# A decoder layer on one core: four pipeline stages instead of five, with the router in attention's iteration

## The chip, the cores and the metric

The kernel runs on one core of one Trainium2 chip. The metric is the device time of one execution in microseconds (us); smaller is better. The engines are PE (TensorE, matmuls), ACT (ScalarE), DVE (VectorE), POOL (GpSimd) and SP (SyncE, which issues all DMAs here). Each engine works through its own list of instructions in order; they meet at semaphores.

## The reference

For 16 batches of 512 tokens with 512 channels, three post-layernorm sublayers follow each other. The linear attention sums along the tokens; the cross attention is one over channels (scores of 128x128 channels in each of 4 heads, twice, with "global" and "local" weights); the feed-forward picks one of 8 experts for a whole batch from the mean of its tokens.

```python
# L0_attn: q, k, v = split(x @ Wqkv.T + bqkv); q, k = elu(scale * .) + 1
denom = clip(einsum('bthd,bthd->bth', q, cumsum(k)), 1e-3)
y = q * cumsum(k * v) / denom
x = layernorm(x + y @ Wproj.T + bproj)
# L0_xattn, for both sets of weights: q = x*wq + bq, k = ctx*wk + bk, v = ctx*wv + bv
scores = einsum('bhdn,bhen->bhde', qh, kh) * 512 ** -0.5
att = einsum('bhde,bhen->bhdn', softmax(scores), vh)
x = layernorm(x + 2.0 * (att_global + att_local) * wp + bp)
# L0_ffn
top1 = argmax(x.mean(axis=1) @ Wr + br)          # one expert for a batch
h = relu(x @ W1[top1] + b1[top1])                # 512 x 2048
x = layernorm(x + h @ W2[top1] + b2[top1])
```

## The kernel before, in words

All products of the linear attention and the feed-forward are split: an operand is a high part (fp32r, copied by ACT) and a low part (the difference, by DVE), and a product of 128 contraction rows is three matmuls hi*hi, hi*lo, lo*hi of 128x512. A group of 12 such matmuls makes one `qkv` job, one `project` tile, one `up` or one `down`.

The kernel is a software pipeline over batches. Iteration i works on five batches at once: stage a (batch i, linear attention), c (i-1, cross attention), e (i-2, router and the transposes of its x), b (i-3, feed-forward) and z (i-4, last sums and layernorm, store). There are NB+4 = 20 iterations. An iteration has 32 halves h. In even halves PE runs `up(b, h//2)` (weights of one 128-wide piece of the hidden layer), in odd ones `down(b, h//2-1)` (half 1: `down(z, 15)`). Ahead of it in each half stands what the function `mix(i, h)` of that engine lists by hand: the 12 qkv jobs (3 for each of four channel blocks, at JOB_AT), gram and the sums for the scores, the transposed attention, and so on. Each of PE, ACT and DVE has such a `mix`; POOL has one list for an iteration, and SP one by halves. So the order on every engine is fixed by the text of these lists, and only semaphores tie them together.

Buffers: X[n] holds a batch's tokens from its load to its store, four of them (NX); the expert's weight pieces have NW = 3 split buffers and NR = 2 raw ones; `xT_hi`/`xT_lo` hold x and later y, `x2T_hi`/`x2T_lo` the feed-forward's input; PSUM has M0, M1 (jobs, projections, denominators, reciprocals), M2 (all of cross attention and router), H_PS and four accumulators.

Names used later. DVE: `keys`, `values` (with two scans), `queries`, `numerator`; `scores_inner` (L672), `scores_ctx` (L677 to L683), `token_sums`, `scores_bias`, `scores_max`; `weigh(c, v)` (L711 to L738, ends with the sum of both a_v); `residual1/2/3`, `statistics`, `moments`; `low_part` (L621, y_lo); `choose` (the expert's index); `split_w` (L760, we_lo); `hidden` (L768, h_lo). ACT: `feature` (L381, L382), `normalise` (L396), `exps`, `split_w` (L424), `split_x2` (L417), `high_part` (L401), `hidden` (L434, L439). POOL: `diagonal` (L311), `rstd_of` (four small operations), `tile_sum` (L305, L308), the additions of b2 (L320), of the projection's bias (L338) and of const_b (L350). PE: `gram` (L944), `ctx_sums` (L951), `x_sums`, `means` (L969), `route`, `attention_T` (L985), `constants` (L992), `attend` (L1003), `denominator` (L903), `spread_reciprocal` (L916), `transpose_x2` (L1019).

## Time and profile before

| | |
|---|---|
| median of 3 runs | 2568.96 us (2568.95 to 2569.8) |
| the profiled execution | 2571.94 us, span 2570.2 us |
| busy: PE / DVE / ACT / POOL | 95% / 68% / 46% / 21% of the span |
| weight loads (PEld), beside the matmuls | 77% |
| mean granted TensorE clock | 0.975 |
| DMA | 331.85 MB, mean 129 GB/s |

The span goes from the first to the last instruction of the profiled execution; the execution's own time is 1.74 us longer. The views used are the page's busy shares, the busy time of each engine in chosen stretches, the timeline of an engine (instructions in order of time, with the idle time before one and who ended it), the groups of equal instructions, and the list of who waited for whom.

### The profile page before, as it was taken

How to read it: one execution, taken by the hardware profiler on the slowest of the kernel's cores; microseconds unless marked ns; L12 is line 12 of the kernel's file. 1: busy time of each engine (PE TensorE's matmuls, PEld its weight loads, DVE VectorE, ACT ScalarE, POOL GpSimd, SP SyncE). 2: the span in 40 equal slices, each digit the busy share in tenths (PEclk: the TensorE clock that was granted, in tenths of full speed). 3: DMA queues.
4: the chain of work that ended last, by engine and by line, in shares of the span. 5: the costliest groups of instructions: out<-in, count | busy, mean ns of one | idle time of the engine just before them, and what ended most of it. 6: DMA issues, size and time to landing. Idle time of an engine off the chain costs nothing.

```text
span 2570.2 us, 33240 instructions
## 1 busy us (share of the span) xinstructions
PE 2430.1 (95%) x11584; PEld 1988.8 (77%) x11584; DVE 1747.5 (68%) x2721; ACT 1172.2 (46%) x1920; POOL 533.6 (21%) x452
## 2 busy tenths in 40 slices
PE   6866899999999999999999999999999999999998
PEld 5655688878788787878878787887878888877876
DVE  6567576677767677676767768667776767765443
ACT  4223444545444443554544455454545445354543
POOL 3132212122112212221122122212212221222110
PEclk9877899999999999999999999999999999999999
DMA  7333333433434344343433434343343434222332
GB/s 274 113 109 107 127 141 117 140 136 108 172 103 159 116 139 145 106 156 119 156 119 121 150 124 160 112 146 128 115 158 117 156 114 145 95 82 87 115 108 69
DMA packets 83400, 331.85 MB, mean 129 GB/s; under 512 B 11810, under 2 KB 11810, under 8 KB 72738
## 3 DMA queue, kind: packets, MB, share of 16 engines
q1 hardware_dynamic: 83234, 329.72, 37.4%
q8 instruction: 94, 1.54, 0.2%
q14 instruction: 72, 0.59, 0.1%
HBM read 306.61 MB, written 23.07 MB: 128 GB/s over the span
## 4 chain that ended last, share of the span: by engine, by line
PE 81%; DVE 10%; ACT 4%; issue 3%; DMA 1%; POOL 1%; SPq 0%; ACTq 0%; DVEq 0%; POOLq 0%
PE m L868 25%; PE acc L1045 24%; PE h_ps L868 23%; DVE junk_v L722 3%; PE m L1003 2%; PE m L944 2%; DVE a_v L726 2%; ACT const_b L465 1%; PE m L1019 1%; PE m L916 1%; PE m L951 1%; DVE h_lo L768 1%; POOL diag L311 1%; PE m L992 1%; ACT rden_all L506 1%
## 5 line engine op out<-in xcount | busy, mean ns | idle before, releaser
L868 PE MATMUL m<-xT_hi,wq 128*128 128x512 f32 x1536 | 514.2, 399 | 24.8 <-DVE wq L550 10.7
L424 ACT ACTIVATE we_hi<-raw 128x1024 fp32r<-128x1024 f32 x256 | 270.7, 1058 | 505.4 <-PE acc L1045 500.3
L760 DVE TENSOR_TENSOR we_lo<-raw,we_hi 128x1024 fp32r<-128x1024 f32 x256 | 368.7, 1440 | 177.6 <-ACT we_hi L424 177.6
L1045 PE MATMUL acc<-we_hi,h_hi 128*128 128x512 f32 x1024 | 423.3, 413 | 0.4
L868 PE MATMUL h_ps<-x2T_hi,we_hi 128*128 128x512 f32 x1024 | 403.4, 394 | 6.0 <-DVE x2T_lo L754 6.0
L1045 PE MATMUL acc<-we_hi,h_lo 128*128 128x512 f32 x1024 | 400.8, 391 | 0.0
L1045 PE MATMUL acc<-we_lo,h_hi 128*128 128x512 f32 x1024 | 400.5, 391 | 0.0
L868 PE MATMUL h_ps<-x2T_lo,we_hi 128*128 128x512 f32 x1024 | 399.6, 390 | 0.0
L868 PE MATMUL h_ps<-x2T_hi,we_lo 128*128 128x512 f32 x1024 | 399.6, 390 | 0.0
L434 ACT ACTIVATE hid<-h_ps,b 128x512 f32<-128x512 f32 x256 | 175.7, 686 | 458.5 <-PE h_ps L868 458.5
L868 PEld LDWEIGHTS m<-xT_hi,wq 128*128 128x128 f32 x1536 | 295.2, 192 | 91.1 <-issue 28.0
L768 DVE TENSOR_TENSOR h_lo<-hid,h_hi 128x512 fp32r<-128x512 f32 x256 | 182.9, 714 | 253.1 <-ACT h_hi L439 252.9
L868 PE MATMUL m<-xT_lo,wq 128*128 128x512 f32 x768 | 304.3, 396 | 0.0
L1045 PEld LDWEIGHTS acc<-we_hi,h_hi 128*128 128x128 f32 x1024 | 193.4, 189 | 49.1 <-issue 9.6
L868 PEld LDWEIGHTS h_ps<-x2T_hi,we_hi 128*128 128x128 f32 x1024 | 192.7, 188 | 45.7 <-DVE x2T_lo L754 6.7
L1045 PEld LDWEIGHTS acc<-we_lo,h_hi 128*128 128x128 f32 x1024 | 193.5, 189 | 43.4 <-issue 7.0
L1045 PEld LDWEIGHTS acc<-we_hi,h_lo 128*128 128x128 f32 x1024 | 192.9, 188 | 42.3
L868 PEld LDWEIGHTS h_ps<-x2T_hi,we_lo 128*128 128x128 f32 x1024 | 192.8, 188 | 40.4
L868 PEld LDWEIGHTS h_ps<-x2T_lo,we_hi 128*128 128x128 f32 x1024 | 192.9, 188 | 38.6
L381 ACT ACTIVATE e_f<-m,sb_qkv,scale 128x512 f32<-128x512 f32 x128 | 99.9, 780 | 220.8 <-PE m L868 217.5
L338 POOL TENSOR_TENSOR x<-x,rows 128x2048 f32<-128x2048 f32 x16 | 74.1, 4629 | 544.4 <-DMA x<-in_x_tok 544.4
L868 PEld LDWEIGHTS m<-xT_lo,wq 128*128 128x128 f32 x768 | 147.9, 193 | 31.3 <-issue 1.0
(126 smaller groups left out, 3480.4 us busy)
## 6 DMA issues: line engine op xcount, KB each, us to landing
raw<-in_w SPq DMA_DIRECT2D x256, 512.0 KB, 3.8
wq<-wq_scratch SPq DMA_DIRECT2D x180, 512.0 KB, 3.3
xT_raw<-in_xT SPq DMA_DIRECT2D x16, 1024.0 KB, 5.9
x<-in_x_tok SPq DMA_DIRECT2D x16, 1024.0 KB, 5.4
ctx_tok<-in_ctx_tok SPq DMA_DIRECT2D x16, 1024.0 KB, 4.9
ctx_T<-in_ctxT SPq DMA_DIRECT2D x16, 1024.0 KB, 4.9
out_dram<-x SPq DMA_DIRECT2D x16, 1024.0 KB, 4.8
wq_scratch<-wq SPq DMA_DIRECT2D x12, 512.0 KB, 4.5
```

The lines of the kernel that those rows point to most:

```text
L338: pool.tensor_tensor(X[a % NX][:, :, :], X[a % NX][:, :, :], rows[:, BPROJ:BPROJ + 1, :].broadcast_to([P, TT, C]), ALU.add).then_inc(xb_do ...
L381: act.activation(e_f[:, :], ps[:, :], ACT.Exp, bias=sb_qkv[:, col:col + 1], scale=scale[:, 0:1]).then_inc(done, 1)
L424: act.activation(we_hi[:, g % NW, :], raw[:, g % NR, :], ACT.Copy).then_inc(whi_done, 1)
L434: act.activation(hid[:, f % 2, :], H_PS[:, :], ACT.Relu, bias=b1[:, b % 2, f:f + 1]).then_inc(h_done, 1)
L722: dve.scalar_tensor_tensor(junk_v[:, h % 2, :], s_a[:, v, h, :], e_rec2[:, v, h:h + 1], rows[:, bv, h * P:h * P + P], ALU.mult, ALU.mult, ...
L726: dve.scalar_tensor_tensor(a_v[:, v, h, :], s_a[:, v, h, :], e_rec2[:, v, h:h + 1], rows[:, wv, h * P:h * P + P], ALU.mult, ALU.mult).then ...
L760: dve.tensor_tensor(we_lo[:, g % NW, :], raw[:, g % NR, :], we_hi[:, g % NW, :].bitcast(F32), ALU.subtract).then_inc(wlo_done, 1)
L768: dve.tensor_tensor(h_lo[:, f % 2, :], hid[:, f % 2, :], h_hi[:, f % 2, :].bitcast(F32), ALU.subtract).then_inc(hlo_done, 1)
L868: last = pe.matmul(out, lhsT, rhs, start=(n == 0), stop=(n == 3 * len(pairs) - 1))
L944: last = pe.matmul(by_head[:, h, :], X[c % NX][:, t, hs], ctx_tok[:, t, hs], start=(t == 0), stop=(t == TT - 1))
L1003: last = pe.matmul(M2[:, h * P:h * P + P], ctx_T[:, h, t * P:t * P + P], aT[:, h, :], start=True, stop=True)
L1045: last = pe.matmul(acc[t][:, :], hx[:, f % 2, ts], wx[:, g % NW, C:], start=(f == 0 and n == 0), stop=(f == FC - 1 and n == 2))
```

## The change

Router (e) and cross attention (c) of a batch come into one iteration: c is batch i-1, b is i-2, z is i-3, and there are NB+3 = 19 iterations. To make room for the chain, cross attention moves to the front of the iteration (gram at half 1, weigh at 8 and 9, attend at 13 to 16, its layernorm at 19) and the router behind it (means 22, route 24, choose 25). The qkv jobs leave halves 7 to 9 free. The sum of the context's channels (ACT) and its diagonal (POOL) are made one iteration earlier. What stood behind the jobs in stage a moves back by one or two halves. A batch's X buffer is free one iteration earlier, so there are three; the weight pieces get four split buffers. `qkv` and `up` now wait for their input part by part instead of for all of it. The order of POOL's list changes with it.

```diff
-NW = 3
-NX = 4
-JOB_AT = [4 * cc + n for cc in range(CC) for n in range(3)]
+NW = 4
+NX = 3
+JOB_AT = [0, 1, 2, 4, 5, 6, 10, 11, 12, 14, 15, 16]
 def stages(i):
-    return i, i - 1, i - 2, i - 3, i - 4
+    return i, i - 1, i - 2, i - 3
...
@@ SP @@
-                    if h == 11 and inside(z):
+                    if h == 13 and inside(z):
                         sp.wait_ge(norm_done, TT * z + TT)
                         sp.dma_start(out[z], X[z % NX][:, :, :]).then_inc(stored, 16)
-                    if h == 15 and inside(a):
+                    if h == 17 and inside(a):
...
-                    if h == 18 and inside(a + 1):
+                    if h == 20 and inside(a + 1):
...
-                    if h == 23 and inside(a):
+                    if h == 25 and inside(a):
...
-                    if h == 26 and inside(a):
+                    if h == 18 and inside(a):
...
                         sp.dma_start(ctx_T[:, :, :], d["ctxT"][a]).then_inc(ctxT_in, 16)
-                    if h == 26 and inside(e):
-                        sp.wait_ge(idx_done, e + 1)
+                    if h == 26 and inside(c):
+                        sp.wait_ge(idx_done, c + 1)
...
@@ POOL: b2 addition of b, then @@
+                    pool.wait_ge(kall2_done, c + 1)
+                    pool.wait_ge(c_mm, c + 1)
+                    diagonal(k_all2, diag2_done)
                 if inside(z):
                     rstd_of(2, z)
                 if inside(c):
                     pool.wait_ge(kb_done, c + 1)
...
                     rstd_of(1, c)
+                    pool.wait_ge(x2_done, TT * c + TT)
+                    pool.wait_ge(sx_mm, c + 1)
+                    tile_sum(c, x2sum_done)
                 if inside(a):
+                    pool.wait_ge(xtok_in, 16 * a + 16)
+                    pool.tensor_tensor(X[a % NX][:, :, :], X[a % NX][:, :, :],
+                                       rows[:, BPROJ:BPROJ + 1, :].broadcast_to([P, TT, C]), ALU.add).then_inc(xb_done, 1)
+                    pool.wait_ge(csum_done, XH * a + XH)
...
+                    diagonal(c_col, diag_done)
                     rstd_of(0, a)
                     pool.wait_ge(x1_done, TT * a + TT)
...
                     tile_sum(a, xsum_done)
@@ ACT, mix: c_sb 5 -> 3, s_x 7 -> 4, exps 13, 15 -> 7, 8; aT 19 -> 11; kb 21 -> 12; normalise(2) 10 -> 12 @@
+                if h == 19 and inside(c):
+                    normalise(1, c)
+                if h == 20 and inside(a):
                     act.wait_ge(rden_done, 3 * a + 3)
...
+                if h == 26 and inside(a):
+                    act.wait_ge(ctxT_in, 16 * a + 16)
...
+                        act.activation(const_b[:, :], ctx_T[:, hd, :], ACT.Copy,
+                                       accum_out=c_col[:, hd:hd + 1]).then_inc(csum_done, 1)
-                if h == 27 and inside(a + 1):
+                if h == 29 and inside(a + 1):
                     split_x(a + 1)
-                if h == 30 and inside(a):
+                if h == 31 and inside(c):
+                    for j in range(3):
+                        split_x2(c, j)
+                if h == 31 and inside(a):
                     normalise(0, a)
@@ DVE, mix @@
+                if h - 1 in JOB_AT and inside(a):
+                    cc, part = divmod(JOB_AT.index(h - 1), 3)
+                    if part == 0:
+                        keys(a, cc)
+                    if part == 1:
+                        values(a, cc)
+                    if part == 2:
+                        queries(a, cc)
+                        numerator(a, cc)
+                if h == 2 and inside(c):
+                    scores_inner(c)
                 if h == 4 and inside(c):
+                    scores_ctx(c)
+                if h == 5 and inside(c):
+                    token_sums(c)
+                    scores_bias(c)
+                if h == 6 and inside(c):
+                    scores_max(c)
+                if h == 8 and inside(z):
                     statistics(2, z, 0)
                     statistics(2, z, 1)
+                if h == 8 and inside(c):
+                    weigh(c, 0)
+                if h == 9 and inside(c):
+                    weigh(c, 1)
...
+                if 14 <= h <= 17 and inside(c):
+                    residual2(c, h - 14)
+                    statistics(1, c, h - 14)
+                if h == 17 and inside(c):
+                    moments(1, c)
...
-                if h == 18 and inside(a):
+                if h == 20 and inside(a):
                     denominator(a)
...
-                if h == 22 and inside(a):
+                if h == 23 and inside(a):
                     for cc in range(CC):
                         low_part(a, cc)
+                if h == 25 and inside(c):
+                    choose(c)
+                if 26 <= h <= 29 and inside(a):
+                    residual1(a, h - 26)
+                    statistics(0, a, h - 26)
...
@@ PE @@
-                if j == 0:
-                    pe.wait_ge(xhi_done, 2 * a + 2)
-                    pe.wait_ge(xlo_done, 2 * a + 2)
...
+                for t in range(CC):
+                    if j == 0 and t % 2 == 0:
+                        pe.wait_ge(xhi_done, 2 * a + t // 2 + 1)
+                        pe.wait_ge(xlo_done, 2 * a + t // 2 + 1)
...
             def up(b, f):
                 g = FC * b + f
-                if f == 0:
-                    pe.wait_ge(x2lo_done, CC * b + CC)
...
+                for j in range(CC):
+                    js = slice(j * P, j * P + P)
+                    if f == 0:
+                        pe.wait_ge(x2lo_done, CC * b + j + 1)
...
@@ PE, mix @@
-                if h == 2 and inside(c):
+                if h == 1 and inside(c):
                     gram(c)
-                if h == 5 and inside(c):
+                if h == 3 and inside(c):
                     ctx_sums(c)
-                if h == 7 and inside(c):
+                if h == 4 and inside(c):
                     x_sums(c)
-                if h == 9 and inside(e):
-                    means(e)
-                if h == 11 and inside(e):
-                    route(e)
-                if h == 17 and inside(a):
+                if h == 11 and inside(c):
+                    attention_T(c)
+                if h == 12 and inside(c):
+                    constants(c)
+                if 13 <= h <= 16 and inside(c):
+                    attend(c, h - 13)
+                if h == 19 and inside(a):
...
+                if h in (21, 22) and inside(a):
+                    spread_reciprocal(a, 2 * (h - 21))
+                    spread_reciprocal(a, 2 * (h - 21) + 1)
+                if h == 22 and inside(c):
+                    means(c)
+                if h == 24 and inside(c):
+                    route(c)
+                if 25 <= h <= 28 and inside(a):
+                    project(a, h - 25)
```

## Rows read from the trace of the kernel before

**Rows 1.** The page: busy shares, and the granted clock in 40 slices.
```profile
PE 2430.1 (95%) x11584; PEld 1988.8 (77%) x11584; DVE 1747.5 (68%) x2721; ACT 1172.2 (46%) x1920; POOL 533.6 (21%) x452
...
PEclk9877899999999999999999999999999999999999
```
**Rows 2.** Stretches: length, busy us (instructions) of each engine, clock, DMA share, GB/s.
```profile
0.00:84.20 84.20, 56.10 (x228) 43.82 (x229) 51.45 (x73) 30.07 (x44) 23.14 (x39) 0.90 0.63 235
84.20:179.30 95.10, 70.60 (x308) 54.92 (x309) 65.79 (x116) 27.82 (x58) 21.90 (x19) 0.81 0.32 111
179.30:286.20 106.90, 76.49 (x341) 59.95 (x341) 70.13 (x125) 36.72 (x72) 29.14 (x26) 0.79 0.35 116
286.20:2258.50 1972.30, 1937.81 (x9398) 1592.92 (x9397) 1406.87 (x2182) 936.09 (x1541) 415.20 (x335) 1.00 0.39 132
2258.50:2370.80 112.30, 106.23 (x497) 86.66 (x497) 68.04 (x118) 52.73 (x90) 24.29 (x20) 0.95 0.27 87
2370.80:2463.40 92.60, 90.62 (x417) 74.82 (x416) 41.62 (x54) 45.55 (x61) 11.67 (x8) 1.00 0.33 106
2463.40:2552.10 88.70, 86.72 (x378) 71.45 (x377) 37.48 (x44) 38.93 (x50) 6.61 (x5) 0.98 0.27 89
2552.10:2570.20 18.10, 5.56 (x25) 4.28 (x23) 6.08 (x13) 4.25 (x6) 1.61 (x4) 0.71 0.14 59
```
**Rows 3.** Timeline of PE in iteration i=8: start, us, instruction, idle before.
```profile
1075.73 0.39 PE L868 MATMUL m<-xT_hi,wq 128*128 128x512 f32 x1
1076.21 1.13 PE L951 MATMUL m<-diag,ones 128*128 128x512 f32 x2
...
1140.38 0.66 PE L985 MATMUL m<-ident,a_v 128*128 128x128 f32 x4 [0.88 <-DVE a_v L738]
...
1156.95 0.47 PE L868 MATMUL m<-wp_hi,xT_hi 128*128 128x512 f32 x1 [1.61 <-issue]
1157.26 0.39 PE L868 MATMUL m<-wp_lo,xT_hi 128*128 128x512 f32 x1
...
1192.42 1.47 PE L1019 MATMUL m<-ident,x 128*128 128x128 f32 x12
...
1197.03 0.47 PE L868 MATMUL m<-xT_hi,wq 128*128 128x512 f32 x1
```
**Rows 4.** Groups of DVE and POOL by form: busy us, mean ns, idle before.
```profile
L768 DVE TENSOR_TENSOR h_lo<-hid,h_hi 128x512 fp32r<-128x512 f32 x256 | 182.9, 714 | 253.1 <-ACT h_hi L439 252.9
L578 DVE TENSOR_TENSOR_SCAN kv_sum<-kv_sum 128x512 f32<-128x512 f32 x64 | 82.7, 1292 | 0.0
...
L308 POOL TENSOR_TENSOR x_sum<-x_sum,x 128x512 f32<-128x512 f32 x64 | 95.2, 1487 | 5.0
```
**Rows 5.** Timelines of DVE, POOL and ACT in iteration i=8.
```profile
1153.43 3.42 DVE L621 TENSOR_TENSOR xT_lo<-ctx_tok,xT_hi 128x512 fp32r<-128x512 f32 x2 [2.44 <-ACT xT_hi L401]
...
1199.03 5.03 DVE L760 TENSOR_TENSOR we_lo<-raw,we_hi 128x1024 fp32r<-128x1024 f32 x1
...
1197.92 5.05 POOL L320 TENSOR_TENSOR x<-x,b 128x2048 f32<-128x2048 f32 x1
...
1190.92 2.92 ACT L396 ACTIVATE x<-x,shift,rstd 128x512 f32<-128x512 f32 x4
...
1197.73 0.58 ACT L417 ACTIVATE x2T_hi<-m 128x512 fp32r<-128x512 f32 x1
```
**Rows 6.** DMA issues: KB each, median us to landing.
```profile
out_dram<-x SPq DMA_DIRECT2D x16, 1024.0 KB, 4.8
```
**Rows 7.** Who PE waited for, 84.20 to 179.30 us (i=1): total, times, longest.
```profile
PE m L985 <- DVE a_v L738: 7.7, 1, 7.7
...
PE m L951 <- POOL diag L311: 2.9, 1, 2.9
```
**Rows 8.** The same, 179.30 to 286.20 us (i=2).
```profile
PE m L1019 <- DVE x2T_lo L754: 9.9, 1, 9.9
```
**Rows 9.** The same, 2258.50 to 2370.80 us (i=16).
```profile
PE m L951 <- POOL diag L311: 3.8, 1, 3.8
```

More of the change, by code:

```diff
@@ L203, in _ @@
             sp.dma_start(X[NX - 1][:, :, :].rearrange("p t n -> p (t n)"), d["w_proj"]).then_inc(wp_in, 16)
-            for i in range(NB + 4):
-                a, c, e, b, z = stages(i)
+            for i in range(NB + 3):
+                a, c, b, z = stages(i)
                 for h in range(HALVES):
@@ L312, in diagonal @@
                                    col[:, :].unsqueeze(2).broadcast_to([P, XH, P]), ALU.mult).then_inc(done, 1)
-            for i in range(NB + 4):
-                a, c, e, b, z = stages(i)
+            for i in range(NB + 3):
+                a, c, b, z = stages(i)
                 if inside(b):
@@ L344, in _ @@
                     diagonal(k_all2, diag2_done)
+                if inside(z):
+                    rstd_of(2, z)
+                if inside(c):
                     pool.wait_ge(kb_done, c + 1)
@@ L441, in mix @@
             def mix(i, h):
[L442 removed]
+                a, c, b, z = stages(i)
                 if h == 0 and inside(b):
@@ L448, in mix @@
                         split_job(j + NQ - 1)
-                if h in (0, 4, 8, 12) and inside(a):
-                    feature(a, h // 4, 0)
-                if h in (2, 6, 10, 14) and inside(a):
-                    feature(a, h // 4, 1)
-                if h == 3 and inside(e):
-                    normalise(1, e)
-                if h == 4 and inside(c):
-                    act.wait_ge(ctxT_in, 16 * c + 16)
-                    if (due := upto(c - 1, 1, 1)) is not None:
-                        act.wait_ge(diag_done, due)
-                    if (due := upto(c - 1, TT, TT)) is not None:
-                        act.wait_ge(x1c_done, due)
-                    for hd in range(XH):
-                        if (due := upto(c, XH, hd)) is not None:
-                            act.wait_ge(csum_done, due)
-                        act.activation(const_b[:, :], ctx_T[:, hd, :], ACT.Copy,
-                                       accum_out=c_col[:, hd:hd + 1]).then_inc(csum_done, 1)
-                if h == 5 and inside(c):
+                if h in JOB_AT and inside(a):
+                    j = JOB_AT.index(h)
+                    if j % 3 != 1:
+                        feature(a, j // 3, j % 3 // 2)
+                if h == 3 and inside(c):
                     act.wait_ge(c_mm, c + 1)
@@ L525, in mix @@
+                if h == 29 and inside(a + 1):
                     split_x(a + 1)
-                if h == 30 and inside(a):
+                if h == 31 and inside(c):
+                    for j in range(3):
+                        split_x2(c, j)
+                if h == 31 and inside(a):
                     normalise(0, a)
-                if h == 31 and inside(e):
-                    for j in range(3):
-                        split_x2(e, j)
             split_x(0)
@@ L535, in _ @@
             act.wait_ge(preset, 4)
-            for i in range(NB + 4):
-                a, c, e, b, z = stages(i)
+            for i in range(NB + 3):
+                a, c, b, z = stages(i)
                 for h in range(HALVES):
@@ L833, in mix @@
                     moments(0, a)
-                if h == 28 and inside(a + 1):
+                if h == 30 and inside(a + 1):
                     split_x(a + 1)
-                if h == 31 and inside(e):
+                if h == 31 and inside(c):
                     for j in range(3):
-                        split_x2(e, j)
+                        split_x2(c, j)
             split_x(0)
@@ L849, in _ @@
             dve.wait_ge(preset, 4)
-            for i in range(NB + 4):
-                a, c, e, b, z = stages(i)
+            for i in range(NB + 3):
+                a, c, b, z = stages(i)
                 for h in range(HALVES):
@@ L1030, in up @@
                     pe.wait_ge(h_done, g)
-                product(H_PS[:, :], [((we_hi[:, g % NW, j * P:j * P + P], we_lo[:, g % NW, j * P:j * P + P]),
-                                      (x2T_hi[:, j, :], x2T_lo[:, j, :])) for j in range(CC)], up_mm)
+                for j in range(CC):
+                    js = slice(j * P, j * P + P)
+                    if f == 0:
+                        pe.wait_ge(x2lo_done, CC * b + j + 1)
+                    pe.matmul(H_PS[:, :], we_hi[:, g % NW, js], x2T_hi[:, j, :], start=(j == 0), stop=False)
+                    pe.matmul(H_PS[:, :], we_hi[:, g % NW, js], x2T_lo[:, j, :], start=False, stop=False)
+                    last = pe.matmul(H_PS[:, :], we_lo[:, g % NW, js], x2T_hi[:, j, :], start=False, stop=(j == CC - 1))
+                last.then_inc(up_mm, 1)
             def down(b, f):
```

179 lines of the change are left out of this document (60 added, 119 removed).

## Prediction

> **What bounds the kernel now.** I read the page's busy shares and clock line first: TensorE (PE) is busy 95% of the span, VectorE (DVE) 68%, and the granted clock is below full only in the first five or so slices and the last [rows 1]. Then I cut the span at the points where PE begins an iteration's half 0 and asked for the busy time of each stretch [rows 2]. The reader is to see three things there. The 13 iterations i=3 to i=15, in which all five stages run, take 1972.30 us, 151.7 each, and PE is busy for 1937.81 of it (98%). The three iterations of the fill (84.20, 95.10 and 106.90 us) have PE busy for 56 to 71 us only, at granted clocks of 0.90, 0.81 and 0.79. The drain has three iterations of 112.30, 92.60 and 88.70 us, in which the feed-forward alone fills PE, and 18.10 us behind the last. So the time is PE's work at full clock, plus what the fill wastes.
>
> Then PE's waits inside one full iteration [rows 3]: before the transposes of L985 it waits 0.88 us for DVE's weigh, before the first projection 1.61 us, and between 1075.96 (0.23, the spacing of two matmuls, after the last one started) and 1076.21 another 0.25 for the diagonal of L951. That is 2.74 us an iteration. I take the 1.61, which the view calls "issue", for the wait on y_lo: the last of DVE's subtractions of L621 ends at 1156.85 and the projection begins at 1156.95 [rows 3, 5]. Twelve matmuls of one product take 12 x 0.227 = 2.72 us, and 48 such groups are 130.6 of the iteration's time.
>
> **1. One iteration goes.** NB+4 iterations become NB+3. Before: three fill, 13 full, three drain. After: two fill, 14 full (i=2 to 15), two drain. The work of all stages stays, so from the stretches [rows 2]: the third fill iteration goes (-106.90), the drain iteration i=17 goes (-92.60), and one full iteration comes in their place. That alone, at 151.7, is -47.8 us.
>
> **2. The full iteration.** Its work on PE is unchanged: the same matmuls, in other halves. I walked the new order through one iteration, each engine in its own order, with the durations of the trace [rows 4], and asked at each PE wait whether its releaser is done.
> - Projection: it moves from half 23 to 25, low_part only from 22 to 23, and attend no longer stands between. y_lo is done about 2.5 us before PE gets there. The 1.61 goes.
> - Attention's diagonal is made in the iteration before (c_col from half 26). The 0.25 goes.
> - attention_T (half 11) waits for weigh (halves 8 and 9). From the end of gram PE has 16 product groups (43.5 us) and some 2 us of small work ahead of it. DVE has, behind residual3, two values of 3.1 us, two queries with numerator of 2.0, four weight splits of 1.2, four h_lo of 0.6, the scores 1.2 + 3.6 + 0.4 + 1.2 + 2.6, statistics 1.2, and weigh 2.5 + 3.6: 33 us (durations as in [rows 4]: 0.6 to 0.7 for 512 elements, 1.2 for a scan or 1024), with about 4 us of waits for ScalarE (ACT) features. It begins 3.6 us behind gram (down(z,15) stands there) and ends 40 us behind it, 5.5 before PE comes. The 0.88 goes.
> - NW=4: ACT's we_hi no longer waits for down(g-3). It is ahead of its reader anyway, so this is nothing by itself, but it frees ACT at half 31, where split_x2 now stands ahead of normalise(0).
> - Iteration boundary: normalise(0) (2.92 us) [rows 5] comes behind the three x2T_hi copies, so the fourth copy is ready about 7.7 us behind the start of the half-31 transposes instead of 5.9 (1192.42 to 1198.31) [rows 3, 5], and its x2T_lo at 8.4. PE needs it at 9.5, since up() now waits part by part (job 0 starts at 4.6, up at 7.4, its fourth part 2.0 later). Covered by 1.1 us; without the part-wise wait it would cost 1.0.
> - POOL's tile sum and its 5 us bias addition start 4.7 us later and fall on halves 0 to 1. DVE's we_lo, with both inputs in SBUF, lasts 5.03 us beside POOL's addition instead of 1.2 [rows 5]; h_lo(0) now meets it, and ends 17.2 behind the transposes; down(0) needs it at 25. residual3 reads PSUM and follows PE. scores_inner ends at 24.3 and ctx_sums, which waits for it, comes at 24.6: covered by 0.3 only. That is the tightest place.
> - Router chain: residual2's last tile at half 17, POOL's four small operations 1.6 us, normalise(1) 2.9, tile sum 4.0 end about 40.5 us behind job 8, means (half 22) comes at 43.6; choose at half 25, and SP needs the index at 26.
> - SyncE (SP): the store at half 13 and the x load at 17 for the buffer just stored leave the store 20 us, it takes 4.8 [rows 6]. All issues keep their number; raw loads still wait for wlo, two splits back.
> - The waits inside two product groups are met when PE arrives. Their price is not in the trace: below, nothing; above, the 0.08 by which a first matmul behind another operation is longer than the 0.23 spacing (1156.95 to 1157.26 is 0.31) [rows 3], eight times an iteration, 0.6 us or 9 in all. I take nothing.
>
> So a full iteration loses 2.74 us: the mean of 151.7 becomes 149.0 (the first, which lacks a down, and the last, which lacks two of the waits, are in the mean), and 14 x 149.0 = 2086.
>
> **3. The fill iteration i=1** now holds attention and router of batch 0 with no feed-forward for cover. Before, it took 95.10 us with 24.5 idle [rows 2], the longest waits 7.7 for weigh, the diagonal's 2.9 [rows 7]. Walked through the new order: job 0 starts 1 us earlier (half of x is enough), the diagonal's 2.9 goes, attention_T waits 6.7 (jobs 6 and 7 are its only cover), kb 1.3, the denominator 2, the spread 5.4 (normalise(1) stands ahead of it on ACT), the projection 5.5 (POOL's x addition blocks low_part), and transposes plus the split of x2T 4.8. That is 25.7 idle, and 1.2 us of means and route more: 97. The 9.9 us for raw weights that stood in the old i=2 [rows 8] goes, because the index is out at 162 and no ctx_T load stands ahead of it on SP. Half 0 of i=2 comes at 181 instead of 286.2.
>
> **4. Drain.** i=16 (112.30) keeps PE's 106.23 of work at a clock of 0.95. The diagonal's 3.8 goes [rows 9]; the wait for x2T_lo before the first up grows by 0.9; the front chain with product groups for only cover is just done in time, and I put 1 to 2 us there. 109.5. Then 88.70 and 18.10 as before.
>
> **Sum** against the profiled span of 2570.2: 84.2 + 97 + 2086 + 109.5 + 88.7 + 18.1 = 2483.5, or -86.7. The profiled execution took 2571.94 (1.74 around the span), and the median of the three runs is 2568.96, 2.98 below it. 2483.5 + 1.74 - 2.98 = 2482.3; I say 2483.
>
> **Two rules against the trace.** The row first: DVE's we_lo lasted as long as POOL's operation [rows 5]. The Trainium skill (SBUF — State Buffer, "SBUF: two separate sides") says that the port pair of the two is a lock held for the whole instruction by whichever began, and that the other fully blocks; by that rule the trace agrees, and what I call covered by 0.3 turns into a wait of up to one POOL operation if POOL wins once more. That is rival 3's mechanism, priced there from rows. And the fill's clock of 0.79 to 0.81 stands where PE idles [rows 2, 7]; the Trainium skill (TensorE: Matmul & The Clock Gate, "What's actually happening") makes the low clock the default that only activity lifts. By it the idle places of the new i=1 would cost twice, which is rival 2.
>
> **Rivals.**
> 1. The waits are moved, not removed: each full iteration meets new ones of about the old sum (ctx_sums for scores_inner, means for the tile sum, down for an h_lo behind POOL). For it: 0.3 and 1.1 us of cover. Against: PE reached 98% with a fuller second half. Time: 2483 + 14 x 2.74 = 2521. Chance 0.20.
> 2. The fill chain is longer, as PE idles in many short pieces and runs more of its 71 us at the low level: 12 matmuls at 1.2 GHz cost 2.7 more. At a mean clock of 0.70 instead of 0.81 the busy part grows by 71 x (0.81/0.70 - 1) = 11, and some 4 us of chain: 2498. Chance 0.15.
> 3. Slower: the DVE front is overfull. Two POOL additions of 5 us fall into the stretch from residual3 to weigh each iteration and PE stands at ctx_sums and attention_T. It decides from a loss of 86.7/14 = 6.2 us an iteration, that is with the chain 11.7 late at attention_T. With both additions fully in series, 10 us at ctx_sums: 2483 + 14 x 9.7 = 2619. Against: only one large addition falls there; the x addition comes behind the router's tile sum. Chance 0.04.
> 4. The fusion does nothing for the span: the lost iteration comes back because i=1 becomes as long as two (190) and the full iterations stay. 2483 + 93 + 38 would be 2614, near rival 3; every wait in i=1 would have to double. Chance 0.02.
>
> **Numbers.** My own case has 0.59, within 2474 to 2495. The range reaches from 15 us below (9 if i=1 meets a third less idle time than I walked, 3 for i=16 without the waits I put there, 3 for the gap of profile and median) over rivals 2 and 1 to half-way between rival 1 and both together: 2468 to 2530. About 0.2% (5 us) is what a measurement of this kernel can tell from no change. Faster holds my case and rivals 1 and 2, 0.94; of the 0.06 of rivals 3 and 4 a hundredth falls within 0.2%: same 0.01, slower 0.05.
>
> **What would show it.** Right: half 0 of i=2 at 178 to 186 us, gram to gram 149.0 to 149.6 (the mean of 149.0 holds the shorter first one), no wait at L985 or before the first projection in full iterations, a PE busy share of 97%. Wrong first at ctx_sums (waiting for s_a of L672), at means (for x_sum), or at i=1 beyond 100 us.

## The result, and the profile after

The changed kernel takes 2461.6 us (median of 4, 2459.3 to 2462.3) against 2569.2 of the kernel before, run on the same chip: ratio 0.958, interval 0.957 to 0.959. That is 107.5 us less. The forecast was 2483 with a range of 2468 to 2530: the sign and the size class were right, the time came out 21 us below the forecast and 6 below the range. Its profiled execution has a span of 2459.6 us.

The page after, busy shares and granted clock (of before: [rows 1]):

```profile
PE 2387.3 (97%) x11584; PEld 1977.4 (80%) x11584; DVE 1737.4 (71%) x2721; ACT 1148.0 (47%) x1920; POOL 560.8 (23%) x452
...
PEclk9889999999999999999999999999999999999999
```

The stretches of the changed kernel, cut near half 0 of i=1, at PE's half 0 of i=2, i=16 and i=17, and behind the last iteration (of before: [rows 2]). The first cut, 81.80, lies inside a wait: PE begins half 0 of i=1 at 84.60, against 84.20 before, so from half 0 to half 0 that iteration takes 98.2:

```profile
0.00:81.80 81.80, 55.72 (x228) 43.61 (x228) 47.39 (x66) 30.85 (x51) 22.00 (x38) 0.90 0.65 241
81.80:182.84 101.04, 71.67 (x341) 56.99 (x341) 70.50 (x133) 35.65 (x71) 29.85 (x25) 0.84 0.34 118
182.84:2250.07 2067.23, 2067.23 (x10123) 1718.55 (x10122) 1512.83 (x2353) 989.05 (x1661) 474.64 (x360) 1.00 0.40 136
2250.07:2355.90 105.83, 102.02 (x497) 83.69 (x496) 62.77 (x116) 51.60 (x85) 25.58 (x20) 1.00 0.29 93
2355.90:2441.38 85.48, 85.09 (x377) 70.20 (x376) 37.81 (x44) 36.58 (x49) 7.12 (x5) 1.00 0.29 93
2441.38:2459.60 18.22, 5.60 (x25) 4.32 (x23) 6.08 (x13) 4.25 (x6) 1.60 (x4) 0.78 0.14 58
```

In the 14 full iterations PE's busy time is the whole stretch, and the list of its waits has no row there. Against the terms of the forecast: half 0 of i=2 comes at 182.8 (forecast 181, +1.8; 0.4 of it is the later start), the full iterations take 2067.2 (2086, -18.8), i=16 takes 105.8 (109.5, -3.7), i=17 85.5 (88.7, -3.2), the rest 18.2 (18.1). Those differences add up to -23.8, and the span's 2459.6 is 23.9 below the sum's 2483.5. So one term carries four fifths of the miss. The forecast also took 2.98 off for the gap between the profiled execution and the median. This time the median lies 0.4 above the profiled execution, and that hides 3.3 us of the miss.

Below, the *step* is the distance in a trace from the first matmul of gram in one full iteration to that of the next. It is 151.96 before and 147.82 after, each to 0.1 in nearly every iteration. The change takes 4.14 us from it. The forecast took 2.74.

The transposed attention in a full iteration, PE's timeline after (of before: [rows 3]): its four transposes follow the last matmul of the job by 0.23, the spacing of two matmuls.

```profile
1272.80 0.39 PE L892 MATMUL m<-xT_hi,wq 128*128 128x512 f32 x1
1273.03 0.60 PE L978 MATMUL m<-ident,a_v 128*128 128x128 f32 x4
1273.38 0.48 PE L1040 MATMUL acc<-we_hi,h_hi 128*128 128x512 f32 x1
```

The fill iteration i=1, who PE waited for (total, times, longest), is close to what was walked:

```profile
PE m L978 <- DVE a_v L733: 7.9, 1, 7.9
PE m L914 <- ACT rden_all L494: 5.8, 1, 5.8
PE m L862 <- issue: 4.4, 1, 4.4
PE m L1010 <- DVE x2T_lo L749: 3.9, 1, 3.9
```

The forecast had 6.7, 5.4, 5.5 and 4.8. The view does not say which of these hides another one behind it; runs 8, 12 and 13 do.

### The profile page after: what moved, and what is told of

Read it like the earlier page. It is cut to its first block, busy times and chain, and to the rows that moved or that the text cites. A ratio compares the mean times of both kernels' runs of the same rounds, so it can differ in the third digit from the quotient of the medians.

```text
span 2459.6 us, 33255 instructions
## 1 busy us (share of the span) xinstructions
PE 2387.3 (97%) x11584; PEld 1977.4 (80%) x11584; DVE 1737.4 (71%) x2721; ACT 1148.0 (47%) x1920; POOL 560.8 (23%) x452
## 4 chain that ended last, share of the span: by engine, by line
PE 94%; DVE 2%; ACT 1%; issue 1%; DMA 1%; POOL 1%; ACTq 0%; POOLq 0%; DVEq 0%; SPq 0%
PE acc L1040 28%; PE h_ps L1024 10%; PE h_ps L1026 9%; PE h_ps L1025 9%; PE m L862 7%; PE m L890 7%; PE m L891 7%; PE m L892 7%; PE m L942 2%; PE m L996 2%; PE m L901 2%; PE m L1010 1%; PE m L914 1%; PE m L964 1%; PE m L949 1%
## 5 line engine op out<-in xcount | busy, mean ns | idle before, releaser
L763 DVE TENSOR_TENSOR h_lo<-hid,h_hi 128x512 fp32r<-128x512 f32 x256 | 299.6, 1170 | 266.5 <-ACT h_hi L434 266.0
L1024 PE MATMUL h_ps<-x2T_hi,we_hi 128*128 128x512 f32 x1024 | 412.4, 403 | 1.7 <-DVE x2T_lo L749 1.3
L1040 PE MATMUL acc<-we_hi,h_hi 128*128 128x512 f32 x1024 | 413.1, 403 | 0.0
L755 DVE TENSOR_TENSOR we_lo<-raw,we_hi 128x1024 fp32r<-128x1024 f32 x256 | 326.9, 1277 | 23.0 <-ACT we_hi L419 22.8
L890 PE MATMUL m<-xT_hi,wq 128*128 128x512 f32 x768 | 304.9, 397 | 17.6 <-DVE wq L545 11.4
L891 PE MATMUL m<-xT_lo,wq 128*128 128x512 f32 x768 | 301.8, 393 | 0.0
L892 PE MATMUL m<-xT_hi,wq 128*128 128x512 f32 x768 | 301.7, 393 | 0.0
L890 PEld LDWEIGHTS m<-xT_hi,wq 128*128 128x128 f32 x768 | 146.2, 190 | 48.8 <-issue 19.0
L295 POOL TENSOR_TENSOR var_e<-mv,ln_eps 128x4 f32<-128x4 f32 x48 | 29.2, 608 | 653.2 <-DVE mv L632 653.2
```

Source lines behind the costliest of these rows:

```text
L755: dve.tensor_tensor(we_lo[:, g % NW, :], raw[:, g % NR, :], we_hi[:, g % NW, :].bitcast(F32), ALU.subtract).then_inc(wlo_done, 1)
L763: dve.tensor_tensor(h_lo[:, f % 2, :], hid[:, f % 2, :], h_hi[:, f % 2, :].bitcast(F32), ALU.subtract).then_inc(hlo_done, 1)
L890: pe.matmul(AB[j % 2][:, :], w[:, 0, t, :], xT_hi[:, t, :], start=(t == 0), stop=False)
L891: pe.matmul(AB[j % 2][:, :], w[:, 0, t, :], xT_lo[:, t, :], start=False, stop=False)
L892: last = pe.matmul(AB[j % 2][:, :], w[:, 1, t, :], xT_hi[:, t, :], start=False, stop=(t == CC - 1))
L1024: pe.matmul(H_PS[:, :], we_hi[:, g % NW, js], x2T_hi[:, j, :], start=(j == 0), stop=False)
```

## The experiments

### Is the 4.14 made of the three waits? PE's order in the kernel before

Run 1 moves all three waiting places by one half; runs 2 and 3 move one each.

```diff
-                if h == 5 and inside(c):        # run 1: ctx_sums and c_sb
+                if h == 6 and inside(c):
-                if h == 19 and inside(c):       # runs 1, 3: attention_T and aT
+                if h == 20 and inside(c):
-                if 23 <= h <= 26 and inside(a): # runs 1, 2: project; residual1,
-                    project(a, h - 23)          # statistics, moments, split_x
+                if 24 <= h <= 27 and inside(a): # one half later too
+                    project(a, h - 24)
```

Run 1: 

> The kernel before, five stages, with PE's three waits of a full iteration taken away by order alone: attention_T and its copy one half later, project with all that follows it one half later, ctx_sums with its copy one half later. By my theory (a wait costs what the view shows plus the time in which matmuls around it go slower, 4.16 us an iteration in the two traces instead of 2.74) the distance from gram to gram falls from 151.97 to 147.8 and the time by 52 to 58 us, to 2511 to 2517. By the rival (a wait costs only what the view shows, and the other 1.4 us came from the part-wise waits or the fourth weight buffer) the distance is 149.2 and the time 35 to 40 lower, 2529 to 2534.

Run 2: 

> The kernel before with project and what follows it one half later, nothing else. The wait shown before it is 1.61 us. If only what is shown counts: 13 x 1.61 = 21 us, 2548. By my theory the product group around the wait lasted 4.59 instead of 2.82, so 13 x 1.77 to 1.9 = 23 to 25 us, 2544 to 2546. The distance from gram to gram is 150.36 by the one and 150.1 to 150.2 by the other.

Run 3: 

> The kernel before with attention_T and its copy one half later, nothing else. The wait shown is 0.88 us: if only that counts, 13 x 0.88 = 11 us, 2558, and gram to gram 151.1. By my theory the up ahead of it (3.76 against 2.72), the transposes (0.70 against 0.36) and the down behind (3.09 against 2.85) all get faster, 1.6 us an iteration: 21 us, 2548, gram to gram 150.35.

Measured: 2586.8 (ratio 1.008, 1.006 to 1.009), 2606.3 (1.015, 1.013 to 1.016) and 2568.4 (1.000, 0.999 to 1.001); steps of 153.4 to 156.0, 153.6 to 156.5, and 152.07. Every theory that I had put down was wrong: no run was faster beyond the noise. Who PE waited for in one full iteration of run 3, and in the whole of run 2:

```profile
PE m L868 <- issue: 1.6, 1, 1.6
PE acc L1045 <- DVE h_lo L768: 1.6, 1, 1.6
```

```profile
PE m L1003 <- DVE x L649: 48.1, 16, 3.3
```

In run 3 the wait at attention_T is gone and the next `down` waits 1.6 for h_lo, which stands behind weigh on DVE. In run 2 the wait before the projection is gone and attend waits 3.3 in each full iteration for residual2, which stands behind low_part on DVE and which the late projection had covered. So PE's order did not make the waits. DVE was late, and whoever came first found it so. The long DVE operations that "Who made DVE late" explains are still there: one of 4.65 in weigh in run 3, and 3.42 for two xT_lo in run 2. That is rival 1 of the prediction ("moved, not removed"), in the kernel before.

### The part-wise waits and the fourth weight buffer

Run 4 puts the part-wise waits alone into the kernel before. Run 7 takes them out of the changed kernel, and run 6 takes out the fourth weight buffer.

```diff
@@ runs 4 (in) and 7 (out), up; qkv likewise with xhi_done, xlo_done @@
-                if f == 0:
-                    pe.wait_ge(x2lo_done, CC * b + CC)
+                    if f == 0:
+                        pe.wait_ge(x2lo_done, CC * b + j + 1)
@@ run 6, from the changed kernel @@
-NW = 4
+NW = 3
```

Run 4: 

> The kernel before with the part-wise waits in qkv and up alone; four stages, buffers and order are not touched. By my theory they give nothing in full iterations (gram to gram 151.97 stays), 1 us in each fill iteration and 1 to 2 in each drain iteration: 4 to 8 us in all, 2561 to 2565. By the rival (they, not the waits, are where the unforecast 1.4 us an iteration comes from) gram to gram is 150.6 and the time 18 to 25 lower, 2544 to 2551. A price of the extra waits, if they have one, would show as gram to gram above 151.97.

Run 7: 

> The changed kernel with the waits for x and x2T in one piece ahead of the product group, as in the kernel before. The prediction put 1.0 us an iteration on it (x2T_lo ready at 8.4, up beginning at 7.4): 14 us and some 3 more in fill and drain, 2478. If the fourth copy comes earlier than walked, full iterations stay at 147.8 and only fill and drain lose, 2464 to 2468. The run of the part-wise waits alone in the kernel before gave them a price of about 0.1 us in a full iteration, so the effect there can also be -0.1.

Run 6: 

> The changed kernel with three split weight buffers in place of four. By the prediction's step (the fourth frees ScalarE at the boundary alone) full iterations stay at 147.8 or gain at most the 0.4 of an uncovered fourth x2T copy, and the time is 2461 to 2468. By the rival (the fourth buffer made the unforecast 1.4 us an iteration) gram to gram is 149.2 and the time 2480. In the two iterations behind the last full one each theory expects a wait before the first up to be back, 2 to 4 us in all.

Measured: run 4 2557.1 (0.996, 0.994 to 0.997), 12 less where 4 to 8 were expected, step 152.07; run 7 2482.6 (against the changed kernel's 2461.6: +20.9), step 148.73; run 6 2461.7, step 147.84. The fourth buffer is worth nothing, in full iterations or in the drain. The part-wise waits cost 0.1 a step in the old order, where nothing is late, and save 0.91 in the new one, where the fourth x2T_lo is. The prediction's "without the part-wise wait it would cost 1.0" was close. PE in run 7:

```profile
1225.45 0.39 PE L892 MATMUL m<-xT_hi,wq 128*128 128x512 f32 x1
1226.52 0.47 PE L1024 MATMUL h_ps<-x2T_hi,we_hi 128*128 128x512 f32 x1 [0.68 <-DVE x2T_lo L749]
```

The rest of their 20.9 us is fill and drain. The last step before i=16 is 148.45 in run 7 and 143.91 in the changed kernel: there the wait is 3.4 us, and the clock granted from 2266 to 2275 is 0.62. In run 4 the drain from the last gram on is 6.0 shorter than before (295.8 against 301.8) and the step before it 3.6 shorter. The forecast's "88.70 as before" for i=17 overlooked this: before, x2T_lo was waited for in each of these iterations.

### The stage count by itself

Run 5 keeps the changed kernel's order of halves but puts the feed-forward one iteration later, with `stages` returning i, i-1, i-3, i-4, NX = 4, NW = 3, NB+4 iterations, and the transposes of x2 and the load of the expert's index for batch i-2.

Run 5: 

> The changed kernel with its order of halves kept, but the feed-forward one iteration later: five stages, 20 iterations, four x buffers and three weight buffers, as before. It splits the gain into the stage count and the order. My sum: one full iteration (147.8) turns into a fill iteration of 95 to 100 and a drain iteration of about 90, so 38 to 43 us above the changed kernel's 2461.6, 2500 to 2505, and gram to gram stays 147.8. The order alone would then be worth 2569 - 2502 = 67 us, where the prediction had 38. By the rival (the shorter iteration needs four stages or four weight buffers) gram to gram is over 149 and the time over 2518.

Measured: 2495.5 (0.972, 0.971 to 0.974), step 147.83. So the order and the part-wise waits give 72 to 74 us at five stages, and the stage count 33.8 by the medians, where the prediction had -47.8 for it and -39 for all the rest. By the gram distances a step of 147.8 is exchanged for a fill iteration of 92.4 (91.92 + 100.84 - 100.39) and 91.9 in the drain, which makes 36.5; the two profiles differ by 3.6 in their starts (first gram at 88.2 and 91.8), so take 34 to 37. The -47.8 was too large because of the old third fill iteration (106.9), which had 9.9 us of waiting for weights in it. The old full iteration of 151.7 worked the other way: with 147.8 in its place the same sum would have given -51.7.

### How much does a wait cost?

In the changed kernel attention_T's input is ready 5.0 us before PE comes (a_v ends at 1268.06, T starts at 1273.03). Runs 10 and 11 take three and two product groups of that cover away, and nothing else.

```diff
-                if h == 11 and inside(c):
-                    attention_T(c)
+                if h == 10 and inside(c) and i > 1:  # run 10: ahead of the job of
+                    attention_T(c)                   # half 10; run 11: behind it
```

Run 10: 

> A wait of known size, put into the changed kernel: from i=2 on the transposed attention stands at half 10 ahead of the job instead of at half 11, and nothing else moves. In the changed kernel its input is ready 5.0 us before it begins, and three product groups are taken from that cover: a shown wait of 2.9 to 3.3 in each of 14 full iterations. If a wait costs what is shown: gram to gram 150.7 to 151.1, 2502 to 2508. If it costs 0.3 to 0.7 more, as the traces of before and after had it: 151.1 to 151.8, 2507 to 2517, and where the granted clock halves behind it, as it did behind some of the 3.3 us waits of the first experiment, another 2.6 us in those iterations.

Run 11: 

> The same with two product groups taken: from i=2 on the transposed attention stands at half 10 behind the job. Shown wait 0.2 to 0.6 in each full iteration. If a wait costs what is shown: gram to gram 148.0 to 148.4, 2464 to 2470. If it costs 0.3 to 0.7 more however short it is: 148.4 to 149.0, 2470 to 2479.

Measured: run 10 2521.1, steps of 151.1 and 152.7 in turn; run 11 2469.8, step 148.39. A row of each:

```profile
1144.07 0.66 PE L978 MATMUL m<-ident,a_v 128*128 128x128 f32 x4 [3.09 <-DVE a_v L733]
```

```profile
1270.30 0.66 PE L978 MATMUL m<-ident,a_v 128*128 128x128 f32 x4 [0.39 <-DVE a_v L733]
```

Shown 3.09, cost 3.30 (151.12 - 147.82; the steps without a fallen clock). Shown 0.39, cost 0.57. Shown 0.68 (run 7), cost 0.91, and up to 0.1 more if the part-wise waits have the same price here as in run 4. In these three runs a wait costs what the timeline shows and 0.2 to 0.3 us more, whatever its length: a matmul's row lasts 0.39 although the next starts 0.23 behind it, so the first 0.16 of each idle time lies under the modelled end, and the first instruction behind is some hundredths slower. My expectation of 0.3 to 0.7 was too high. It explains some 0.6 of the missing 1.4 and not the rest. The waits of the weight loads' queue (PEld) point to the rest. One full iteration, before and then after:

```profile
PEld m L868 <- issue: 2.0, 1, 2.0
PEld m L985 <- DVE a_v L738: 1.3, 1, 1.3
PEld acc L1045 <- issue: 1.2, 5, 0.2
PEld m L916 <- ACT rden_all L506: 0.5, 1, 0.5
PEld m L951 <- POOL diag L311: 0.5, 1, 0.5
PEld m L975 <- issue: 0.4, 1, 0.4
PEld m L903 <- issue: 0.4, 1, 0.4
PEld acc L1045 <- ACT h_hi L439: 0.2, 1, 0.2
```

```profile
PEld acc L1040 <- issue: 0.7, 3, 0.2
PEld m L901 <- issue: 0.4, 1, 0.4
PEld m L970 <- issue: 0.4, 1, 0.4
PEld h_ps L1024 <- issue: 0.2, 1, 0.2
PEld h_ps L1025 <- issue: 0.2, 1, 0.2
```

The "issue" rows of 0.2 to 0.4 behind short matmuls are in both; 6.5 against 1.9 leaves 4.6, in which each wait is about 0.2 too long (3.5 for the 3.30 of run 10). The reader is to see two entries that the forecast lacks: the spread for rden_all, and the `down` behind attention_T for h_hi.

The distances from one matmul's start to the next settle it, summed at each place in one iteration before (1210.74 to 1362.70) and set against the same places in the changed kernel. Attention_T and the `down` behind it lose 1.30 (forecast 0.88), the first projection 1.85 (1.61), the diagonal 0.37 (0.25), the spread 0.36 (0), the transposes of x2 0.17 (0). That is 4.05 of the 4.14. Of the missing 1.4, some 0.8 is what the three known waits cost beyond what was summed for them, and 0.5 is two places that were not in the sum.

Run 9 closes the gap in the jobs (`JOB_AT = [4 * cc + n ...]` as before).

Run 9: 

> The changed kernel with the qkv jobs at the halves of the kernel before (0 to 2, 4 to 6, 8 to 10, 12 to 14): the gap of halves 7 to 9, in which weigh runs, is closed. If DVE's backlog around weigh is what made the waits of the kernel before (its h_lo and attention's sum behind 6 us of weigh and the values' scans), one of them is back: gram to gram 148.5 to 150.5, 2471 to 2499. If the place of weigh ahead of job 8's work is enough, 147.8 stays and the time is 2459 to 2464.

Measured: 2472.0 (0.962, 0.960 to 0.963), step 148.66. Attention_T still does not wait; attend waits 0.6 for residual2, which stands behind the values' scans on DVE. The gap is worth 0.8 a step.

### Who made DVE late

The rows of iteration i=8 ahead of the prediction show we_lo beside GpSimd (POOL) [rows 5] but not these, DVE and then POOL:

```profile
1129.00 0.35 DVE L722 SCALAR_TENSOR_TENSOR junk_v<-s_a,e_rec,rows 128x128 f32<-128x128 f32 x1
...
1129.28 4.65 DVE L722 SCALAR_TENSOR_TENSOR junk_v<-s_a,e_rec,rows 128x128 f32<-128x128 f32 x1
```

```profile
1129.11 4.66 POOL L338 TENSOR_TENSOR x<-x,rows 128x2048 f32<-128x2048 f32 x1 [34.70 <-DMA x<-in_x_tok]
...
1150.63 5.67 POOL L350 TENSOR_TENSOR x<-x,const_b 128x512 f32<-128x512 f32 x4 [11.17 <-ACT const_b L520]
```

One 128x128 operation of weigh lasts 4.65 instead of 0.35: it ends 0.2 behind POOL's bias addition. And the two xT_lo that take 3.42 instead of 1.3 [rows 5] lie beside POOL's four const_b additions. These are the releasers of the two long waits. Runs 14 to 16 change POOL's list alone, in the kernel before.

```diff
@@ run 15 and 16: const_b additions behind y_lo @@
+                    if inside(a):
+                        pool.wait_ge(ylo_done, CC * a + CC)
                     pool.wait_ge(kb_done, c + 1)
@@ run 14 and 16: x + projection's bias behind the const_b additions @@
-                if inside(a):
-                    pool.wait_ge(xtok_in, 16 * a + 16)
-                    pool.tensor_tensor(X[a % NX][:, :, :], ...).then_inc(xb_done, 1)
...
                         pool.tensor_tensor(X[c % NX][:, t, :], ..., const_b[:, :], ALU.add)...
+                if inside(a):
+                    pool.wait_ge(xtok_in, 16 * a + 16)
+                    pool.tensor_tensor(X[a % NX][:, :, :], ...).then_inc(xb_done, 1)
```

Run 14: 

> The kernel before with one GpSimd operation at another place of its list: the 4.66 us addition of the projection's bias to x (at 1129.11 in i=8, where a 128x128 operation of weigh on DVE lasts 4.65 us instead of 0.35) goes behind the additions of const_b. New theory: the wait at attention_T (0.88 shown, 1.6 us by the distances of the groups around it) is this collision, not DVE's own work: weigh ends 4.3 us earlier, the wait goes, gram to gram 150.3 to 150.5, 2546 to 2551. Rival: the wait moves to an h_lo, as it did when PE's order was changed, or to the projection, which grows: 151.5 to 152, 2562 to 2570.

Run 15: 

> The kernel before with GpSimd's four additions of const_b (5.67 us at 1150.63 in i=8) held back until y_lo is done (a wait on ylo_done). New theory: the 1.61 before the first projection is two xT_lo that took 3.42 us beside them instead of 1.3; y_lo is done at 1154.8 and PE comes at 1155.3. The wait goes: gram to gram 150.0 to 150.3, 2543 to 2548. Rival: the additions come late for residual2 and attend waits for it, as when the projection was moved: 151 to 153, 2556 to 2582.

Run 16: 

> Both edits of GpSimd's list in the kernel before: the const_b additions wait for y_lo, and the bias addition follows them. If both waits are collisions with GpSimd, gram to gram is 148.3 to 148.8 (the diagonal's 0.5 and the spread's stay) and the time 2520 to 2528, so that 3.2 to 3.7 of the 4.14 us that the change takes from a full iteration are to be had with five stages and PE's, ScalarE's and DVE's orders untouched. Rival: the bias addition, now at 1160 to 1165, holds up residual1 and the third projection: 149.5 to 151, 2536 to 2558.

Measured: run 14 2586.5 (1.007, 1.005 to 1.009), step 153.58; run 15 2534.8 (0.987, 0.985 to 0.989), step 150.18; run 16 2514.1 (0.979, 0.977 to 0.981), step 148.42. Run 16 takes 3.54 of the 4.14 from the step, with PE, ACT and DVE in their old order and five stages. What is left, 0.60, are the diagonal (0.37) and the transposes (0.2); the spread's loss is gone too. Twelve steps make 42 of the 55 us, and most of the rest is in the fill, whose first two gram distances shrink by 11.1 together. That is why runs 15 and 16 came out 8 and 6 us below their expected times while their steps were as expected. Weigh and y_lo in run 16, DVE and then POOL:

```profile
1248.97 0.35 DVE L725 SCALAR_TENSOR_TENSOR junk_v<-s_a,e_rec,rows 128x128 f32<-128x128 f32 x1
...
1271.37 1.29 DVE L624 TENSOR_TENSOR xT_lo<-ctx_tok,xT_hi 128x512 fp32r<-128x512 f32 x2 [2.43 <-ACT xT_hi L404]
```

```profile
1272.74 6.41 POOL L348 TENSOR_TENSOR x<-x,const_b 128x512 f32<-128x512 f32 x4 [17.89 <-DVE xT_lo L624]
1279.12 4.58 POOL L351 TENSOR_TENSOR x<-x,rows 128x2048 f32<-128x2048 f32 x1
```

Run 14 missed, and shows the same thing from the other side. Attention_T no longer waits there, as expected. But the bias addition now meets we_lo, which stands ahead of residual2, and attend waits 3.07 for it. The collision was moved, not removed:

```profile
1312.38 5.02 POOL L349 TENSOR_TENSOR x<-x,rows 128x2048 f32<-128x2048 f32 x1
```

```profile
1312.89 5.59 DVE L761 TENSOR_TENSOR we_lo<-raw,we_hi 128x1024 fp32r<-128x1024 f32 x1
```

The lock of the port pair that the Trainium skill describes (SBUF — State Buffer, "SBUF: two separate sides") fits all of these rows: DVE's operation ends 0.2 to 1.1 us behind POOL's and not by its own length.

### A better fill

Runs 8, 12 and 13 edit iteration i=1 of the changed kernel alone. Each keeps the edits of the one before.

```diff
@@ run 8: PE, attention_T in i=1 at 12 (was 11); ACT, i=1 @@
+                if h == 20 and i == 1:     # behind rden_all, not at half 19
+                    normalise(1, c)
@@ run 12: in i=1 means at 26, route and choose at 27, m_col at 24 @@
@@ run 13: POOL, ahead of the addition of the projection's bias @@
+                    if i == 1:
+                        pool.wait_ge(ylo_done, CC * a + CC)
```

Run 8: 

> The changed kernel with two edits in iteration i=1 alone: the transposed attention stands behind the ninth job instead of ahead of it, and ScalarE copies the reciprocals (rden_all) before it normalises the cross attention's x instead of after. The waits there are 7.85 and 5.84 us. Mine: 2.7 of the first and some 4 of the second go, and the projection's 4.35 shrinks because the y parts are made ahead of GpSimd's addition; half 0 of i=2 at 175 to 178 instead of 182.8, 2454 to 2457. Rival: the waits move to the means and to the index, and nothing or 1 to 2 us is left, 2460 to 2462.

Run 12: 

> The reordered fill of the eighth experiment, with one thing more in iteration i=1 alone: means, the copy of the mean (m_col), route and choose stand behind the first projection, so that ScalarE's y_hi no longer queues behind the wait for the means. There xT_hi was made at 155.3 behind m_col although the spread was done at 150. Mine: the projection begins at 154 to 156 instead of 162, half 0 of i=2 comes 5 to 7 us earlier than in the eighth experiment, 2451 to 2454. Rival: GpSimd's addition of the projection's bias holds up y_lo or residual1, or the expert's weights come later than the feed-forward, and 0 to 3 us are left, 2456 to 2459.

Run 13: 

> The fill of the twelfth experiment, in which four xT_lo of 0.7 us took 9.6 us beside GpSimd's tile sum and its addition of the projection's bias, with the addition of iteration i=1 held back until y_lo is done. Mine: y_lo at 154.5 to 156 instead of 160.6, the projection 4 to 5 us earlier, the addition done at 160 to 161 when residual1 comes, half 0 of i=2 at 176 to 178: 5 to 7 us under the changed kernel's 2461.6, 2455 to 2457. Rival: what is left there is chain, and the addition now holds up residual1 and through it the third projection by as much: 2458 to 2461.

Measured: 2458.7 (2457.1 to 2462.1), 2460.2 (2458.1 to 2461.6) and 2457.2 (2455.8 to 2458.3). The start of the program, which none of them touches, differs by up to 3.7 us between the profiles (the first gram stands at 88.5 to 92.2), so I read the distance from there to half 0 of i=2: 91.1 in the changed kernel, 90.8 in run 8, 89.6 in run 12, 86.6 in run 13. From gram to gram it is 100.4, 101.1, 99.6 and 96.4. Run 8 gave 0.3 at most and not 5 to 7: xT_hi stood on ACT behind m_col, which waits for the means, which wait for POOL. Run 12 freed it and met the next collision, DVE and then POOL:

```profile
150.99 9.58 DVE L618 TENSOR_TENSOR xT_lo<-ctx_tok,xT_hi 128x512 fp32r<-128x512 f32 x4
```

```profile
151.86 3.26 POOL L308 TENSOR_TENSOR x_sum<-x_sum,x 128x512 f32<-128x512 f32 x2
155.09 4.93 POOL L343 TENSOR_TENSOR x<-x,rows 128x2048 f32<-128x2048 f32 x1
```

With the addition held back (run 13) the four take 5.29, and the fill is 4.5 us shorter than in the changed kernel (4.0 from gram to gram). Run 13 is the fastest kernel here, 2457.2 against 2461.6. Against before its ratio is 0.956 (0.955 to 0.958), which overlaps the changed kernel's, so the 4.4 us rest on the medians and on the distance in the trace.

## Why the prediction missed by its size

- **"So a full iteration loses 2.74 us" is the step that failed.** It measured 4.14, and over the 14 iterations that term is 18.8 of the 21 to 24 us. The three waits were summed as shown. No cost was put on what a wait does beyond its row (some 0.2 each in runs 7, 10 and 11), on the `down` behind attention_T (0.20), on the spread (0.36) or on the transposes (0.17). The mechanism, that the waits go, was right. No row of PE's waits is left.
- **What made the waits was not seen.** I argued from cover on PE's side and from DVE's sum of work, and counted one POOL addition in the front. The cover came out: a_v is ready 5.0 before PE comes (forecast 5.5), y_lo 2.1 (2.5). But shown by runs 14 to 16, the old waits were two collisions of DVE with POOL's additions, so 3.54 of the 4.14 are to be had without the change. In the changed kernel the two big additions of an iteration meet two h_lo with slack instead: of the 256 h_lo the mean is now 1170 ns, 714 before [rows 4], and nobody waits. How much of the 4.14 the missing collisions give there, and how much the greater cover, no run separates; the cover alone exceeds the 4.3 of weigh's collision.
- **Stage count -47.8:** 34 to 37 in the new order (run 5). In the old order it was not measured.
- **Boundary "covered by 1.1; without the part-wise wait 1.0":** 0.91 (run 7). Right.
- **Price of the part-wise waits, taken as 0 between 0 and 0.6:** 0.1 (run 4). Right.
- **NW=4 "nothing by itself":** 147.84 against 147.82 (run 6). Right, and it has no use at the boundary either.
- **i=1 97 us, half 0 of i=2 at 181:** 98.2 from half 0 to half 0, and 182.8. Right, and the diagonal's wait is gone. The parts are off by up to 1.2 each way (7.9 for 6.7, 4.4 for 5.5) and nearly cancel, which is luck.
- **i=16 109.5 and "then 88.70":** 105.8 and 85.5. The gain of the part-wise waits in the drain was left out (runs 4 and 7): the wait before the first up of i=16 was to grow by 0.9, and it shrank from 2.1 to 1.3. The clock there was 1.00 and not the 0.95 that was kept. The terms as written (112.30 - 3.8 + 0.9 + 1 to 2) also add up to 110.4 to 111.4, not to 109.5.
- **Rival 1** (waits moved, 0.20) and **rival 3** (front overfull): no new wait in the full iterations. The tight place "covered by 0.3" held: the h_lo of 4.72 us beside POOL is there, and ctx_sums comes 0.3 behind scores_inner without a wait. **Rival 2** (a longer fill at a clock of 0.70) and **rival 4** (i=1 as long as two): i=1 took 98.2, at a clock of 0.84.

```profile
1222.97 4.72 DVE L763 TENSOR_TENSOR h_lo<-hid,h_hi 128x512 fp32r<-128x512 f32 x1 [0.24 <-ACT h_hi L434]
```

- **The range** had its low end 15 below the forecast, all of it given to fill, drain and the gap of profile and median. The one term that is multiplied by 14 had no room downwards.

## What to carry to other kernels

A wait that repeats in every iteration should be priced by the distance between the groups around it, compared with the same groups where nothing waits, and not by the idle time of its row; ask for the weight loads' waits too. Before moving the engine that waits, look at the duration of each operation ahead of the releaser. Here one lasted thirteen times its usual (4.65 for 0.35) and two lasted two and a half times theirs; both were collisions, and the place to mend was the other engine's list. In the kernel before, two moved additions of GpSimd's list gave 55 us where the whole change gives 107.

## What the runs showed of the hardware that was not expected

A wait can cost the clock as well. Behind attend's wait of 3.30 us in run 1 the granted clock fell in 6 of 12 full iterations, and stayed full in the other 6 behind the same wait. Where it fell longest, the `down` behind lasted 4.64 instead of 2.83 and the step was 2.6 us longer (1.5 in the four milder ones). That iteration, cut around the wait; 0.50 is the level of 1.2 GHz:

```profile
996.00:1002.00 6.00, 3.69 (x21) 2.86 (x19) 4.22 (x3) 3.42 (x5) 4.65 (x4) 0.98 0.01 3
1002.00:1008.00 6.00, 5.01 (x16) 4.34 (x17) 3.61 (x6) 0.00 (x0) 0.00 (x0) 0.50 0.73 262
```

In run 10 a wait of 3.1 us met it in every second iteration (a clock of 0.66 in the 5 us behind, the job 4.42 instead of 2.85, the step 1.6 longer); in run 2 the wait of 3.30 met it in 9 of 12 full iterations, and in run 14 one of 3.07 in only 2 of 12. Behind waits of 0.4 to 1.7 us in full iterations it did not happen. One of 2.07 before the first up of i=16 met it in the kernel before and in runs 1 and 2 (0.72 in the 6 us behind) and not in runs 3, 14 and 15. So the wait of 3.1 us cost 3.3 and, in the mean over the iterations of run 10, 0.8 more for the clock. Why one iteration is hit and the next is not stays open.
